# The heads' diagonal products on the two column halves of the TensorE array

## What is computed

```python
xBC = jax.nn.silu(conv + b_conv[None, :, None]).transpose(0, 2, 1)
X = x.reshape(b, l, NHEADS, HEADDIM)              # 16 heads of 64
L = _segsum_exp(Ab)                               # decay inside a chunk, per head
Y_diag = jnp.einsum('bcln,bcsn,bhcls,bcshp->bclhp', Cb, Bb, L, Xb)
Y_off = jnp.einsum('bcln,bchpn,bhcl->bclhp', Cb, states, state_decay_out)
Y = (Y_diag + Y_off).reshape(b, l, h, p)
```

## Time and profile before

| | |
|---|---|
| time, median of 3 runs (lowest to highest) | 1485.34 us (1485.32 to 1486.46) |
| the profiled execution, its own time | 1485.38 us |
| its span in the profile | 1483.6 us |
| PE busy | 1459.3 us, 98% |
| PEld busy | 1196.4 us, 81% |
| DVE busy | 1121.4 us, 76% |
| mean granted clock of TensorE | 0.996 of full |

### The profile page before, as it was taken

The page is one execution under the profiler, slowest core; times in us unless marked ns, Lnnn a source line. Parts: engine busy times, 40 slices in busy tenths (PEclk is TensorE's granted clock), DMA queues, the critical chain, the costliest instruction groups (busy, mean ns, idle before and its releaser), DMA issues.

```text
span 1483.6 us, 23344 instructions
## 1 busy us (share of the span) xinstructions
PE 1459.3 (98%) x8345; PEld 1196.4 (81%) x8345; DVE 1121.4 (76%) x2521; ACT 637.6 (43%) x1300; POOL 294.3 (20%) x335
## 2 busy tenths in 40 slices
PE   7899999999999999999999999989999999999998
PEld 3688887887887888878878878778888888888887
DVE  4888898898898898988988988965646465464642
ACT  5555565475465565654754655522112021120210
POOL 1012223213212222222132123122111101101011
PEclk9999999999999999999999999999999999999999
DMA  9403213212222132132122221802201202012010
GB/s 328 144 29 129 87 44 125 83 51 93 93 86 93 40 125 93 36 136 93 44 106 74 79 94 61 296 28 86 72 22 64 86 7 79 22 65 85 8 50 30
DMA packets 56401, 124.86 MB, mean 84 GB/s; under 512 B 6438, under 2 KB 10066, under 8 KB 52188
## 3 DMA queue, kind: packets, MB, share of 16 engines
q1 hardware_dynamic: 55744, 123.27, 23.3%
q10 hardware_dynamic: 540, 0.07, 0.0%
HBM read 97.62 MB, written 25.69 MB: 83 GB/s over the span
## 4 chain that ended last, share of the span: by engine, by line
PE 91%; issue 4%; DVE 1%; POOL 1%; DMA 1%; ACT 1%; POOLq 0%; SPq 0%; DVEq 0%
PE bank L1443 28%; PE bank L2029 18%; PE bank L2059 9%; PE bank L1542 7%; PE bank L1591 7%; PE bank L1589 6%; PE bank L1532 4%; PE bank L1554 4%; PE bank L1509 2%; PE bank L1569 2%; PE bank L325 2%; PE bank L1433 1%; PE bank L2010 1%; PE bank L1481 1%; POOL ff_x_resid L1856 1%
## 5 line engine op out<-in xcount | busy, mean ns | idle before, releaser
L1864 ACT ACTIVATE silu_gate<-bank,params 128x512 f32<-128x512 f32 (+1 forms) x99 | 63.5, 642 | 367.3 <-PE bank L2029 346.4
L987 DVE SCALAR_TENSOR_TENSOR xBC<-conv_in,wconv,xBC 128x256 f32<-128x256 f32 x480 | 211.9, 474 | 3.4 <-ACT xBC L697 0.4
L1936 DVE SCALAR_TENSOR_TENSOR hidden<-bank,params,silu_gate 128x512 f32<-128x512 f32 (+1 forms) x99 | 68.3, 690 | 125.4 <-PE bank L2029 124.1
L1542 PEld LDWEIGHTS bank<-X,decay 128*128 128x128 f32 x1024 | 123.1, 192 | 22.8 <-issue 19.4
L2059 PE MATMUL bank<-W_down,hidden_high 128*128 128x512 f32 x374 | 139.1, 390 | 0.0
L606 POOL TENSOR_TENSOR X_D<-X,Drow 128x1024 f32<-128x1024 f32 x32 | 61.9, 1934 | 364.1 <-ACT X_D L781 324.5
L2029 PE MATMUL bank<-ff_h_high,W_gate 128*128 128x512 f32 (+1 forms) x352 | 132.3, 380 | 0.0
L2029 PE MATMUL bank<-ff_h_high,W_up 128*128 128x512 f32 (+1 forms) x352 | 131.1, 377 | 0.4 <-DVE hidden L1936 0.4
L2029 PE MATMUL bank<-ff_h_low,W_gate 128*128 128x512 f32 (+1 forms) x352 | 131.0, 376 | 0.0
L2029 PE MATMUL bank<-ff_h_low,W_up 128*128 128x512 f32 (+1 forms) x352 | 131.0, 376 | 0.0
L2059 PE MATMUL bank<-W_down,hidden_low 128*128 128x512 f32 x330 | 128.5, 389 | 0.0
(11 more groups left out here) (196 smaller groups left out, 3283.4 us busy)
## 6 DMA issues: line engine op xcount, KB each, us to landing
decay<-sums_scratch SPq DMA_DIRECT2D x32, 1024.0 KB, 4.8
wq_rows<-wqT SPq DMA_DIRECT2D x33, 256.0 KB, 4.0
widened_scratch<-wq_rows SPq DMA_DIRECT2D x33, 256.0 KB, 2.3
x_tile<-x SPq DMA_DIRECT2D x32, 256.0 KB, 3.2
x_resid<-x SPq DMA_DIRECT2D x32, 256.0 KB, 3.1
x_scratch<-x_resid SPq DMA_DIRECT2D x32, 256.0 KB, 2.4
ff_x_resid<-x_scratch SPq DMA_DIRECT2D x32, 256.0 KB, 4.6
out<-ff_x_resid SPq DMA_DIRECT2D x32, 256.0 KB, 2.0
```

The source lines that it names most:

```text
L987: nc.vector.scalar_tensor_tensor(A.xc[b][:, m, :], A.raw[:, m, j:j + SC], A.wconv[:, m, j:j + 1], A.xc[b][:, m, :], ALU.mult, ALU.add).the ...
L1542: mm = nc.tensor.matmul(ydiag[:, h * HD:(h + 1) * HD], A.L[c][:, g, :], A.X[:, g * HD:(g + 1) * HD], start=True, stop=True)
L1864: self.nc.scalar.activation(B.sg[m % 2][:, 0:size], self.gates[m % 2][:, 0:size], ACT.Silu, scale=self.T.sgate[:, m:m + 1]).then_inc(self. ...
L1936: nc.vector.scalar_tensor_tensor(hid, self.ups[m % 2][:, 0:size], self.T.sup[:, m:m + 1], B.sg[m % 2][:, 0:size], ALU.mult, ALU.mult).then ...
```

## The change

Each of the 8 products of a group becomes two. The first takes columns 0 to 63 of the scores as weights and writes partitions 0 to 63 of the bank, the second columns 64 to 127 and partitions 64 to 127; `tile_position` puts them on the left and on the right column half of the array. Both stream the same 64 columns of X. Waits, the increment on the last product and all other instructions stay as they are.

```diff
@@ -1539,8 +1539,11 @@
             wait(pe, ydiag_read, u, 2 * NC, 2 * c + f)
             for h in range(HH):
                 g = f * HH + h
-                mm = nc.tensor.matmul(ydiag[:, h * HD:(h + 1) * HD], A.L[c][:, g, :],
-                                      A.X[:, g * HD:(g + 1) * HD], start=True, stop=True)
+                for i in (0, P // 2):
+                    s = slice(i, i + P // 2)
+                    mm = nc.tensor.matmul(ydiag[s, h * HD:(h + 1) * HD], A.L[c][:, g, s],
+                                          A.X[:, g * HD:(g + 1) * HD], start=True, stop=True,
+                                          tile_position=(0, i))
             mm.then_inc(ydiag_done, 1)
```

## The result

The changed kernel took 1462.21 us (median of 4 runs, 1459.53 to 1463.41) against 1485.88 us for the kernel before (4 runs beside it). The ratio is 0.9839, 95% interval 0.9826 to 0.9851. I had forecast 1508 us and slower. The result lies inside my range and on the other side of "no change"; it is my first rival, minus a quarter of its gain (23.7 us instead of 31).

What follows compares the result with a forecast made beforehand. PE was taken as the bound. Per group, two silences of 0.093, loads of 1.79 and a bare stream of 0.054 sum to 2.03 against 1.68 us; 64 groups add 22.5 to 1485.4, giving 1508 us, range 1453 to 1522.

Steps and rivals of the forecast that it cites:

- rival 1: Diagonal products: loads into the two halves run side by side, 17 steps a group, -31 us, 1454 us; chance 0.22.
- What bounds the kernel before: Whole kernel: PE, busy 98% of the span, bounds it; time the diagonal products take or give back moves the end equally.
- The load's pace sets the group: Inside a group: loads, not streams, set the pace; 0.112 us for 128 columns, 0.056 for 64.
- The silence of 0.09 us at each change of size: Entering and leaving each group: PE falls silent 0.093 us at each change of tile size.
- 32 loads x 0.056 = 1.79, one behind the other: In each group: 32 half-width loads run strictly in sequence, none hidden, 1.79 us.
- bounds for the unknown: Two loads into different halves at once: between half of them in parallel and none; none was taken.
- The rival's price: Group with side-by-side loads: 17 x 0.056, plus 0.054 and two silences, 1.19 us, -0.49 a group.
- DVE would allow it: Mixer, under side-by-side loads: DVE, busy 815 us of then 880, would permit the gain.
- rival 2: Small load-product pairs in a group have a floor of 0.061 us instead of 0.056: +10 more, 1518 us; chance 0.12.
- Rival 3: In a group, a load into one half waits for the other half's stream: +52 more, 1560 us; chance 0.06.
- rival 4: Halves are no tiles to the array: no silence, first load stays hidden, +3.6 us, 1489 us; chance 0.05.

Runs made afterwards that it cites:

- e6: The kernel before, without column halves, plus two moves in DVE's order (last softplus steps earlier, first new state's read inside gate): 1485.78 us, ratio 1.0002.
- e8: The kernel before with less work on DVE (L1062 formed for 64 of the 128 columns only): 1485.42 us in one run.
- e4: The change, but the fourth head of each group of eight stays one product on the full array: 1477.35 us, ratio 0.9941.
- e1: The change, reordered so each group does first all 8 left-half products, then all 8 right-half ones: 1499.16 us, ratio 1.0087 to the kernel before.
- e10: e5 with the first two products of cumulate (L1491, L1492) also on column halves: 1456.60 us, ratio 0.9798 to the kernel before.
- e11: e5 with column quarters in the groups and in the first two products of cumulate: 1459.93 us, ratio 0.9822 to the kernel before.
- e5: The change plus two moves in DVE's order (last softplus steps earlier, first new state's read inside gate): 1455.77 us, ratio 0.9802 to the kernel before.
- e3: The change with four products of 32 columns per head, on column quarters instead of halves: 1459.91 us in one run.
- e2: The change with the halves ordered left, left, right, right for every two heads: 1465.55 us in one run.

## Why the prediction was wrong

- **What bounds the kernel before: right.** PE alone: e6 changed DVE's order and e8 took load off it, and neither changed the time. But "a nanosecond that the diagonal products take or give back on PE moves the end by one" holds only as far as the table of turns goes without long turns, down to 57.49 us a turn (e4); at 56.23 it no longer does.
- **The load's pace sets the group, 0.875 ns a column: right.** e1 has 0.057 to 0.058 us for a load of 64 columns, I had 0.056.
- **The silence of 0.09 us at each change of size, two a group: right**, in the change (0.10 on entering), in e4 with two more, and in e10 and e11 where the size stays and they vanish. The doubt whether it belongs to narrow tiles alone is settled: 128 to 64, 64 to 128 and 64 to 32 have it.
- **The step that failed: "32 loads x 0.056 = 1.79, one behind the other".** It is 16 steps of 0.058, 0.93 us. I had set bounds for the unknown (half of them in parallel, none) and took "none, because all rows show that". But all of those rows load one and the same tile; not one of them had two tiles with loads to do, so they could not speak on it either way. The value should have stayed open between its ends, with a chance nearer to a half. That the result lies in my range is owed to the width that rival 1 gave it, not to the forecast.
- **The rival's price: nearly right.** 1.19 us a group was computed, 1.18 measured; the first load also has a partner, so it is 16 steps and not 17. The Trainium skill's sentence in TensorEngine Tiling (Array Packing), Key Properties, that different tiles can load and multiply in parallel, holds: two loads at 425.50. The sentence in TensorE: Matmul & The Clock Gate, Part 3, that loads overlap matmuls in flight only on other rows of the array, does not: both halves use all 128 rows, and steps of 0.058 us leave no room for a load of 0.056 and a stream of 0.054 one behind the other. (The same part, under The mechanism, also lets a load run ahead when it goes to a background weight buffer; with that the rows agree.)
- **What neither the forecast nor the rival had: the end of the gain.** For rival 1 I wrote that DVE would allow it, by its busy time (815 of 880 us). That is a mean. By the medians 8.3 of the 32 us were given back, and 6.1 of them came back with two moves in DVE's order (e5); the other 2.2 lie about where e5's four long turns (1.9 us) put them. Busy shares say whether an engine can do the work, not whether it does each piece in time.
- Floors for small pairs (rival 2) did not bind: load-product pairs came 0.058 us apart within one half (e1), 0.028 in the change and 0.013 in e3. Rival 3 is refuted by the even steps of 0.058 us, rival 4 by the silences.

## What to carry to other kernels

Where a product's stream is shorter than its load (here 64 columns against 128), the load sets the pace, and two column tiles that alternate in the program nearly halve it (0.112 us to 0.058 for the same weights), at 0.09 us for each change of size; keep products of one tile size together, and do not put all products of one tile behind all of the other (e1 was slower than the untiled kernel). A row that shows an operation only in one place cannot price it in two: ask of each row whether it could have shown the other outcome. Once the first engine is relieved (here by 2%), look in its new waits for work of other engines that stands ahead of what it wants, and move that.

## What was new in the hardware's behaviour

- Weight loads for different column tiles run side by side, two at 64 columns (16 steps of 0.058 us for 32 loads) and four at 32 columns (e3, 0.053 us for four), though they use the same 128 rows.
- The look-ahead is short: it bridges two products of the same half (e2, 1.13 us a group against 1.08) but not eight (e1, 1.83 us, pairs only in the last three steps ahead of the border).
- The silence goes with the change of tile size in either direction, also between 64 and 32 columns (e10), and is absent between tiles of one size from different lines (e10, e11).
